# A recurrent scan written out as 64 steps, with the second batch's decay on VectorE

## The reference, cut to what matters

```python
def step(S, ins):                      # S: (batch, head, v, k)
    r_t, w_t, k_t, v_t, a_t, b_t = ins
    Sa = jnp.einsum('bhvk,bhk->bhv', S, a_t)
    S = S * jnp.exp(w_t)[:, :, None, :] + Sa[..., None] * b_t[:, :, None, :] + v_t[..., None] * k_t[:, :, None, :]
    o = jnp.einsum('bhvk,bhk->bhv', S, r_t)
    return (S, o)
```

## Time and profile before

| what | value |
|---|---|
| median of 3 runs (lowest, highest) | 3158.77 us (3151.08, 3159.28) |
| profiled execution, its own time | 3151.4 us |
| profiled execution, its span | 3149.6 us |
| busy shares of the span | PE 85%, DVE 69%, POOL 59%, ACT 44% |
| mean granted TensorE clock (1 is full speed) | 0.923 |

### The profile page before, as it was taken

One profiled execution on the slowest core, in us unless ns is written; L12 is line 12 of the kernel. 1 busy time (PEld: TensorE's weight loads), 2 busy tenths in 40 slices (PEclk: granted clock), 3 DMA queues, 4 the chain that ended last, 5 costly groups with the idle time before them and its releaser, 6 DMA issues. The chain is left out here.

```text
span 3149.6 us, 62893 instructions
## 1 busy us (share of the span) xinstructions
PE 2686.0 (85%) x23924; PEld 1842.2 (58%) x23924; DVE 2164.2 (69%) x3616; ACT 1383.7 (44%) x2041; POOL 1861.9 (59%) x1955
## 2 busy tenths in 40 slices
PE   4777677795999999999888999999534789999997
PEld 2555534553777777777656666666311456666666
DVE  5777346455676767667578888876586588887874
ACT  2122012333666666666524544545322134545454
POOL 0899000002878878787646788887200257888885
PEclk8999778897999999999989999999756899999999
DMA  1000000001110101101010000000000100000000
GB/s 38 1 1 1 1 20 11 21 1 61 25 25 19 29 19 25 24 19 29 3 52 1 2 1 1 2 2 1 17 0 0 53 1 1 2 1 2 1 2 15
DMA packets 31170, 41.72 MB, mean 13 GB/s; under 512 B 10344, under 2 KB 17896, under 8 KB 30880
## 3 DMA queue, kind: packets, MB, share of 16 engines
q1 hardware_dynamic: 30880, 37.76, 4.4%
HBM read 19.91 MB, written 1.05 MB: 7 GB/s over the span
## 5 line engine op out<-in xcount | busy, mean ns | idle before, releaser
L1380 POOL TENSOR_TENSOR at_p_lo<-at_p_t 128x512 bf16<-128x512 f32 x512 | 523.7, 1043 | 159.3 <-ACT at_p_t L1350 127.7
L1886 PE MATMUL banks<-g_w,normed_t 128*128 128x320 f32 x1536 | 501.9, 454 | 30.4 <-DVE g_scratch L2174 30.2
L1350 ACT COPY g_p_t<-banks 128x512 f32<-128x512 f32 x512 | 288.0, 588 | 400.4 <-PE banks L1321 399.5
L2174 DVE TENSOR_TENSOR g_scratch<-banks,g_gate 128x640 f32<-128x640 f32 x384 | 314.1, 821 | 197.5 <-PE banks L1886 194.3
L1368 DVE TENSOR_REDUCE at_negmax<-banks 128x1 f32<-128x1024 f32 x256 | 301.5, 1219 | 213.1 <-PE banks L1299 213.1
L1380 POOL TENSOR_TENSOR g_p_lo<-g_p_t 128x512 bf16<-128x512 f32 x256 | 266.7, 1045 | 150.1 <-ACT g_p_t L1350 127.5
L1886 PEld LDWEIGHTS banks<-g_w,normed_t 128*128 128x128 f32 x1536 | 270.3, 195 | 122.0 <-DVE g_scratch L2174 47.1
L1368 DVE TENSOR_REDUCE g_negmax<-banks 128x1 f32<-128x1024 f32 x256 | 310.3, 1217 | 33.3 <-PE banks L1299 32.9
L1363 ACT ACTIVATE g_p<-banks,g_negmax 128x1024 f32<-128x1024 f32 x256 | 286.2, 1118 | 99.9 <-DVE g_negmax L1368 92.3
L1350 ACT COPY at_p_t<-banks 128x512 f32<-128x512 f32 x384 | 212.3, 588 | 256.5 <-PE banks L1321 251.4
L1321 PEld LDWEIGHTS banks<-identity,g_p 128*128 128x128 f32 x2048 | 235.3, 141 | 138.6 <-issue 115.9
(11 more groups left out here) (391 smaller groups left out, 5828.9 us busy)
## 6 DMA issues: line engine op xcount, KB each, us to landing
at_swapped<-at_crossed SPq DMA_DIRECT2D x256, 64.0 KB, 2.0
g_w<-in_ex_w SPq DMA_DIRECT2D x2, 2880.0 KB, 11.6
f_w<-in_W SPq DMA_DIRECT2D x2, 1024.0 KB, 5.9
at_rope<-in_rope SPq DMA_DIRECT2D x1, 2048.0 KB, 9.1
g_w<-in_ex_w SPq DMA_DIRECT2D x2, 960.0 KB, 5.4
out<-residual SPq DMA_DIRECT2D x1, 1024.0 KB, 5.1
at_w<-in_at_w SPq DMA_DIRECT2D x1, 768.0 KB, 4.5
rw_weights<-in_rw_w SPq DMA_DIRECT2D x1, 512.0 KB, 4.0
```

Of the source, the lines that this page charges most:

```text
L1350: self.nc.scalar.copy(self.pt[:, j % self.deep, h, g * CHUNK:(g + 1) * CHUNK], self.core.ps[self.home(n)]).then_inc(self.pt_copied, 1)
L1380: self.nc.gpsimd.tensor_tensor(self.p_lo[:, j % self.deep, h, part], self.pt[:, j % self.deep, h, part], self.pt_hi[:, j % self.deep, h, p ...
L1886: nc.tensor.matmul(out[:, 0:ED], core.xt[:, at:at + P], w[:, kind * H + tile // (T * BATCH) * 2 + h, :], start=True, stop=True).then_inc(p ...
L2174: v.tensor_tensor(qk_product[:, tile % 2, kind] if kind < 2 else v_product[:, tile % 2], core.banks[:, bank:bank + 2, 0:ED].rearrange("p h ...
```

## The change

1. The loops of all four engines are written out in full, so step numbers, the columns and the numbers in waits become constants.
2. For batch 1 the decay product is no longer made by GpSimd from the SBUF copy of the state but by VectorE from PSUM, straight behind `times_a` (new function `decay`, semaphore `decayed`). GpSimd keeps it for batch 0, and keeps L435 for both.
3. Waits that go with it: GpSimd's add of batch 1 waits for `decayed`; GpSimd waits for the SBUF copy of batch 1 only ahead of L440; ScalarE's copy of batch 1 waits for `decayed` (the decay that reads the same PSUM bank); VectorE's L511 of batch 1 waits for ScalarE's earlier copy (`x_copied`).

```diff
             def copy_state(n, s, b):
                 act.wait_ge(y_ready, n * 2 + b + 3)
+                if b:
+                    act.wait_ge(decayed, min(n + 2, STEPS))
                 nc.scalar.copy(state[:, s % 2, b * PER:(b + 1) * PER], lot(6 + b, s % 2)).then_inc(x_copied, 1)
-            with act.Fori(0, STEPS // BLOCK) as q:
+            for q in range(STEPS // BLOCK):
...
-            with step.loop(STEPS // BLOCK // 2, 2 * BLOCK * 2) as qq:
+            for qq in range(STEPS // BLOCK // 2):
...
-                            pool.wait_ge(x_copied, n * 2 + b + 1)
-                            step(g.tensor_tensor(x1[:, b], before[:, mine], seq["w"][:, mine, bass.ds(n, 1)].to_broadcast([P, PER, ROWS]), ALU.mult))
+                            if b == 0:
+                                pool.wait_ge(x_copied, n * 2 + 1)
+                                step(g.tensor_tensor(x1[:, 0], before[:, mine], seq["w"][:, mine, n:n + 1].to_broadcast([P, PER, ROWS]), ALU.mult))
+                            else:
+                                pool.wait_ge(decayed, n + 1)
                             g.tensor_tensor(x1[:, b, :, 0:K], x1[:, b, :, 0:K],
                                             kv[:, i].rearrange("p v (c s) -> p c v s", s=BLOCK)[:, mine, :, s], ALU.add).then_inc(x1_ready, 1)
                         if s == 1:
                             pool.wait_ge(o_full, q * 2 + 2)
+                        pool.wait_ge(x_copied, n * 2 + 2)
...
+            def decay(n, src):
+                v.tensor_tensor(x1[:, 1], src, seq["w"][:, PER:2 * PER, n:n + 1].to_broadcast([P, PER, ROWS]),
+                                ALU.mult).then_inc(decayed, 1)
...
+            decay(0, state[:, 1, PER:2 * PER])
-            with step.loop(STEPS // BLOCK // 2, 2 * BLOCK * 2) as qq:
+            for qq in range(STEPS // BLOCK // 2):
...
                             dve.wait_ge(x1_ready, n * 2 + b + 1)
+                            if b:
+                                dve.wait_ge(x_copied, n * 2 + 2)
                             v.tensor_tensor(lot(6 + b, s % 2), lot(b, 1), x1[:, b], ALU.add).then_inc(x_ready, 1)
                             dve.wait_ge(x_ready, n * 2 + b + 1)
                             times_a(n + 1, b, lot(6 + b, s % 2))
+                            if b and n + 1 < STEPS:
+                                decay(n + 1, lot(6 + b, s % 2))
```

More of the change, by code:

```diff
@@ L232, in rwkv_stage @@
         y_ready, u_full, x1_ready, x_ready = sem("y_ready"), sem("u_full"), sem("x1_ready"), sem("x_ready")
-        x_copied = sem("x_copied")
+        x_copied, decayed = sem("x_copied"), sem("decayed")
         yr_ready, v_full, kv_ready, o_full, o_copied = (sem(n) for n in ("yr_ready", "v_full", "kv_ready", "o_full", "o_copied"))
@@ L288, in spread_v @@
                 r = s // 2
-                ins = mm(core.ps[2 + r % 2][:, (s % 2) * 256:(s % 2 + 1) * 256], give[:, s, :], seq["v"][:, :, bass.ds(q * BLOCK, BLOCK)],
+                ins = mm(core.ps[2 + r % 2][:, (s % 2) * 256:(s % 2 + 1) * 256], give[:, s, :], seq["v"][:, :, q * BLOCK:(q + 1) * BLOCK],
                          start=True, stop=True)
@@ L305, in _ @@
             pe.sem_inc(o_full, 4)
-            with pe.Fori(0, STEPS // BLOCK // 2) as qq:
+            for qq in range(STEPS // BLOCK // 2):
                 for i in range(2):
@@ L395, in copy_outputs @@
                 act.wait_ge(o_full, q * 2 + i + 5)
-                nc.scalar.copy((o, yc)[i][:, :, bass.ds(q * BLOCK, BLOCK)],
+                nc.scalar.copy((o, yc)[i][:, :, q * BLOCK:(q + 1) * BLOCK],
                                core.ps[4 + i][:, 0:256].rearrange("p (c s) -> p c s", s=BLOCK)).then_inc(o_copied, 1)
@@ L438, in _ @@
                             pool.wait_ge(o_full, q * 2 + 2)
+                        pool.wait_ge(x_copied, n * 2 + 2)
                         j, slot = (i, s - 1) if s else (1 - i, BLOCK - 1)
                         g.tensor_tensor(yr[:, j, :, :, slot].rearrange("p r c -> p c r"), before,
-                                        seq["r"][:, :, bass.ds(n, 1)].to_broadcast([P, COLS, ROWS]), ALU.mult).then_inc(yr_ready, 1)
+                                        seq["r"][:, :, n:n + 1].to_broadcast([P, COLS, ROWS]), ALU.mult).then_inc(yr_ready, 1)
             pool.wait_ge(x_copied, STEPS * 2 + 2)
@@ L487, in key_values @@
                                 core.ps[2 + r % 2].rearrange("p (v c s) -> p v c s", v=2, s=BLOCK),
-                                seq["k"][:, :, bass.ds(q * BLOCK, BLOCK)].unsqueeze(1).to_broadcast([P, 2, COLS, BLOCK]),
+                                seq["k"][:, :, q * BLOCK:(q + 1) * BLOCK].unsqueeze(1).to_broadcast([P, 2, COLS, BLOCK]),
                                 ALU.mult).then_inc(kv_ready, 1)
@@ L492, in times_a @@
                 mine = slice(b * PER, (b + 1) * PER)
-                v.tensor_tensor(ya[:, b], src, seq["a"][:, mine, bass.ds(n, 1)].to_broadcast([P, PER, ROWS]),
+                v.tensor_tensor(ya[:, b], src, seq["a"][:, mine, n:n + 1].to_broadcast([P, PER, ROWS]),
                                 ALU.mult).then_inc(y_ready, 1)
+            def decay(n, src):
+                v.tensor_tensor(x1[:, 1], src, seq["w"][:, PER:2 * PER, n:n + 1].to_broadcast([P, PER, ROWS]),
+                                ALU.mult).then_inc(decayed, 1)
             for r in range(4):
@@ L508, in _ @@
                             dve.wait_ge(u_full, n * 2 + b + 1)
-                            step(v.tensor_tensor(lot(b, 1), lot(b, 0), seq["b"][:, mine, bass.ds(n, 1)].to_broadcast([P, PER, ROWS]), ALU.mult))
+                            step(v.tensor_tensor(lot(b, 1), lot(b, 0), seq["b"][:, mine, n:n + 1].to_broadcast([P, PER, ROWS]), ALU.mult))
                             dve.wait_ge(x1_ready, n * 2 + b + 1)
+                            if b:
+                                dve.wait_ge(x_copied, n * 2 + 2)
                             v.tensor_tensor(lot(6 + b, s % 2), lot(b, 1), x1[:, b], ALU.add).then_inc(x_ready, 1)
```

## The result

| | before | changed kernel |
|---|---|---|
| median of 5 runs each (lowest, highest) | 3158.77 us (3151.08, 3159.99) | 3133.16 us (3126.92, 3138.41) |
| ratio, 95% interval | | 0.9917 (0.9905 to 0.9929) |
| measured again on another occasion (9 runs before, 5 changed) | 3158.24 us (3154.42, 3161.5) | 3135.13 us (3131.62, 3138.68) |
| its ratio, 95% interval | | 0.9929 (0.9915 to 0.9942) |
| profiled execution, own time and span | 3151.4, 3149.6 us | 3129.6, 3127.8 us |

The kernel became 0.8% faster, 26 us by the first ratio, 22 us by the second. The forecast was 16.7 us less, 3142; 0.9917 of 3158.77 is 3132.6, just under the range's low end of 3133. The direction and the bounds of the step were right; the gain was put too small, because one cost was charged that hardly came.

What follows compares the result with a forecast made beforehand. GpSimd's 3.45 us step bounds the scan, then VectorE's 3.16: 64 x 3.16 = 202.2, + 8.5 boundaries + 6.3 clock + 1.0 = 218.0 us against 234.7. That is 16.7 less, 3142 us; range 3133 to 3160.

Steps and rivals of the forecast that it cites:

- What bounds the kernel and what takes over: Scan step: GpSimd bounds it at 3.45 us before the change, VectorE at 3.16 us after.
- The new product at 0.34: VectorE's added decay product costs 0.34 us for each of 64, bounds 0.34 and 0.42.
- The register gap: VectorE, L511 to L493: written out, falls from 0.57 to 0.46 us, twice 0.11 per step.
- The rival of the gap that stays: Gap belongs to the semaphore; VectorE's step stays 3.38, 5 us less, 3154 us; chance 0.12.
- The loop turns: The scan's three loop turns, 6.9 us of VectorE waiting for nothing shown, go when written out.
- the 6.1 us: Old scan's remainder for three loop turns, slow steps behind them and the end; 1.0 of it kept.
- The chains: New copy and GpSimd chains of both batches fit VectorE's step at cost 0; batch 0's put at 2.34 us.
- Boundaries: Block boundaries in the scan: VectorE stalls 1.22 us for GpSimd, seven times, 8.5 us.
- TensorE's clock: Behind block boundaries TensorE's clock falls and its lateness reaches VectorE: 6.3 us, bounds 0 and 9.
- 1.31 - 2 x 0.23, rounded to 0.9 us, seven times: Clock charge per boundary: three slow rows' 1.31 us extra less two steps' 0.23 slack; 6.3 us in all.
- the case that the clock does not bite: Rival: TensorE's clock drop falls on its idle time; 23 us less, 3136 us; chance 0.13.
- The sum: Scan total 202.2 + 8.5 + 6.3 + 1.0 = 218.0 us against 234.7, 16.7 less; kernel 3142 us.

Runs made afterwards that it cites:

- Experiments 1: Changed kernel with all loops written out but batch 1's decay left on GpSimd; 0.9969 of the kernel before, scan 226.4 us.
- experiment 4: Changed kernel with each decay product made twice on VectorE, one into an unread spare tile; 0.9982 of the kernel before, median 3152.4 us, scan 231.4 us.
- experiment 3: As experiment 2, but the product with a always reads fixed column 0; 0.9977 of the kernel before, scan 220.5 us.
- experiment 2: Changed kernel with loops and register arithmetic kept, only batch 1's decay moved to VectorE; 0.998 of the kernel before, scan 233.9 us.
- experiment 7: Changed kernel with GpSimd's kv wait moved to its first add (0.9905 of before), then also key_values between the batches (0.9901, again 0.989).
- experiment 5: Changed kernel with a block's output rows given out 4, 4, 2, 2, 2, 1, 1; single execution 3145.7 us, scan 216.0 us.
- experiment 6: Kernel before and changed kernel run again unchanged: scans 233.9 and 212.2 us; changed kernel 0.9929 of before.

## Why the prediction was off, point by point

- **What bounds the kernel and what takes over: right.** GpSimd at 3.45, then VectorE at 3.16. Experiments 1 and 4 show both.
- **The new product at 0.34: right**, 0.33 in experiment 4, and with it the choice of 0.34 over its whole duration of 0.42.
- **The register gap: right in size and in cause.** 0.57 to 0.46 in the changed kernel; experiment 3 places it in the column's address. The rival of the gap that stays is out. It is more than half of the gain: 64 x 0.22 = 14 us, 13.4 between experiments 2 and 3.
- **The loop turns: right to let them go.** No wait of VectorE for nothing shown took their place in the written-out scan. The prediction's remark that the list has no other such wait over 1.0 us overlooked one of 1.03, ahead of the scan and in every run alike. It also overlooked the second stall of each turn, 1.5 us in all (experiment 2); that changed nothing, as the 6.1 us held both.
- **The chains: right**, at a cost of 0; batch 0's is 2.25 us and not 2.34 (experiment 7).
- **Boundaries: 8.5 us forecast, 7.3 measured** (seven times 1.04). I took over the 0.26 us of GpSimd's wake-up from the loop form; written out it is 0.08, and the 0.18 between them is the whole difference of 1.22 and 1.04.
- **TensorE's clock: this is the term that failed, 6.3 us forecast, 1.9 measured.** The fall itself came, as read from the earlier trace rows, at six of the seven boundaries. The step that failed is "1.31 - 2 x 0.23, rounded to 0.9 us, seven times": it set TensorE's lateness only against the slack of TensorE's own step and left out the lead with which its product is ready ahead of VectorE's use. That lead is 1.36 us where the slow rows fall (0.76 in the other steps), so a lateness of 0.9 would have cost nothing. In fact TensorE was later than I had charged, 9.6 us over the seven boundaries and not 6.3, and the lead took all but 1.9; experiment 5 shows it being used up. I had given the case that the clock does not bite 0.13, and what came is near to it, though not for the reason given there, that the fall lies on TensorE's idle time.
- **The sum.** 202.2 + 7.3 + 1.9 + 0.8 = 212.2, measured 212.4: with the terms at their measured size (0.8 is the end and the first step, put at 1.0) the sum closes within 0.2 us. From 218.0 to 212.4 is 5.6 us more gain; 3142 would have been 3136.4. The other 3.2 us down to 3133.2 are within what two executions of one kernel differ by outside the scan (experiment 6), but are not placed further; on the second occasion the ratio gives 22.4 us, what the scan gained in the first pair. The range's low end allowed 23 us of gain and 3 for scatter; with the two mis-sized terms, 1.2 and 4.4 us, it had no room left.

## What to carry to other kernels

Where two engines bound a loop within a few per cent of each other, find both steps before costing an edit: here each half alone brought 8 and 1 us, and both together 22. Here the address worked out from a loop counter cost nothing beside a running instruction (`times_a` to the next product is 0.34 or 0.35 us in the loop and written out, apart from four to six places of 0.45 to 0.55 in a looped scan) and 0.11 us behind a wait on the critical chain; look for it as two dependent pairs with unequal gaps. Before charging an engine's lateness, subtract the lead with which its result lies ready; it is one subtraction in the timeline.

## What the runs showed that I had not expected

A loop turn of VectorE has two stalls for nothing shown, 2.0 to 2.5 us and, at the other batch of the same step, 0.4 to 0.8 us. Together they are 8.2 to 8.4 us for three turns in the kernel before and in experiments 2 and 3; written out there was none. GpSimd also woke faster in written-out code: 0.08 us behind the instruction that it waited for, against 0.17 behind ScalarE's copy and 0.26 to 0.35 behind `kv` in the loop form. Whether the column or the wait's own number costs that was not separated. And two spans of the same kernel differed by 8 us, all of it outside a scan that repeated within 0.85 us, so in this kernel an edit of a few us is better read from its stretch of the trace than from the total.
